# Expert gates for two of four quarters fetched from DRAM instead of spread by TensorE, in a convolution, attention and expert block

## What is computed

```python
logits = tokens @ router_w.T
probs = softmax(logits)
rw, re = top_k(probs, 2);  rw = rw / rw.sum(-1)
combine = zeros(N, 8);  combine[arange(N), re] = rw
for e in range(8):
    h = gelu(tokens @ w1[e] + b1[e])
    y = h @ w2[e] + b2[e]
    out = out + combine[:, e:e+1] * y
```

## Time and profile before

| what | value |
|---|---|
| median of three runs | 1167.22 us |
| the profiled execution, its own time | 1171.15 us |
| its span in the profile | 1169.3 us |
| TensorE busy | 1100.4 us, 94% |
| VectorE busy | 909.2 us, 78% |
| ScalarE busy | 611.7 us, 52% |
| GpSimd busy | 146.7 us, 13%, nothing of it in stage 3 |
| mean DMA rate | 68 GB/s |
| chain that ended last | TensorE 79%, ScalarE 8%, VectorE 6% |

### The profile page before, as it was taken

How to read it: one execution, slowest core, us unless ns; L and a number is a source line. 1 busy time by engine, 2 the same in 40 slices (tenths; PEclk the granted TensorE clock), 3 DMA queues, 4 the chain that set the end, 5 groups by cost and what they waited for, 6 DMA issues and landing times.

```text
span 1169.3 us, 28068 instructions
## 1 busy us (share of the span) xinstructions
PE 1100.4 (94%) x9550; PEld 739.6 (63%) x9550; DVE 909.2 (78%) x2575; ACT 611.7 (52%) x975; POOL 146.7 (13%) x173
## 2 busy tenths in 40 slices
PE   7858999999999999998789999999999999999998
PEld 7836777777777777777554555555555555555553
DVE  6943678888888888888678887887777777887875
ACT  0014566666666666665245555555555555555553
POOL 6021222222222222222100000000000000000000
PEclk9957899999999999999569999999999999999999
DMA  9501112122121212111012222222222222222221
GB/s 285 212 16 33 49 49 62 52 60 55 57 57 56 58 50 61 53 57 41 24 47 60 67 71 70 67 68 70 71 66 67 71 71 67 68 70 69 67 67 48
DMA packets 136196, 79.18 MB, mean 68 GB/s; under 512 B 112417, under 2 KB 134177, under 8 KB 135345
## 3 DMA queue, kind: packets, MB, share of 16 engines
q1 hardware_dynamic: 127040, 64.78, 21.3%
q10 hardware_dynamic: 8064, 12.85, 2.9%
q0 software_dynamic: 1008, 0.43, 0.2%
HBM read 52.33 MB, written 25.69 MB: 67 GB/s over the span
## 4 chain that ended last, share of the span: by engine, by line
PE 79%; ACT 8%; DVE 6%; issue 3%; SPq 2%; DMA 1%; POOL 0%; DVEq 0%; ACTq 0%; POOLq 0%
PE p L1096 16%; PE p L1071 15%; PE p L1081 9%; PE p L1045 6%; PE p L916 5%; PE p L1011 5%; PE p L1023 4%; ACT prob L515 4%; PE p L909 4%; PE p L926 3%; ACT xt_s L459 3%; PE p L1040 2%; PE p L1092 2%; PE p L924 2%; DVE arena L603 1%
## 5 line engine op out<-in xcount | busy, mean ns | idle before, releaser
L532 ACT ACTIVATE arena<-p,b_s 128x896 f32<-128x896 f32 x224 | 225.3, 1007 | 246.9 <-PE p L1071 246.1
L825 DVE TENSOR_TENSOR arena<-arena,p 128x896 f32<-128x896 f32 x224 | 242.7, 1083 | 93.0 <-PE p L1081 89.8
L1096 PE MATMUL p<-arena,w_s 128*64 128x448 f32 x896 | 215.7, 560 | 0.3 <-DVE arena L825 0.3
L1071 PE MATMUL p<-thl,w_hi 128*128 128x448 f32 x448 | 164.9, 449 | 0.4 <-DVE thl L799 0.4
L1081 PE MATMUL p<-arena,selector 128*128 128x448 bf16 x448 | 124.7, 360 | 3.5 <-DVE arena L825 3.0
L1081 PEld LDWEIGHTS p<-arena,selector 128*128 128x128 bf16 x448 | 25.5, 97 | 161.6 <-issue 116.1
L1071 PE MATMUL p<-thl,w_lo 128*128 128x448 f32 x448 | 127.5, 366 | 0.0
L723 DVE TENSOR_REDUCE sm<-sq 128x14 f32<-128x896 f32 (+1 forms) x59 | 61.3, 1038 | 66.7 <-ACT sq L486 58.7
L1071 PEld LDWEIGHTS p<-thl,w_hi 128*128 128x128 f32 x448 | 85.8, 192 | 21.3 <-issue 1.0
L418 POOL TENSOR_TENSOR yb<-yb,bet 128x448 f32<-128x448 f32 x56 | 59.2, 1058 | 290.5 <-DVE xn_s L766 290.5
L1071 PEld LDWEIGHTS p<-thl,w_lo 128*128 128x128 f32 x448 | 85.0, 190 | 7.2
(11 more groups left out here) (174 smaller groups left out, 1793.8 us busy)
## 6 DMA issues: line engine op xcount, KB each, us to landing
tn_spill<-tnt_s ACTq DMA_DIRECT2D x56, 224.0 KB, 1.9
arena<-tn_spill SPq DMA_DIRECT2D x56, 224.0 KB, 3.4
t_s<-tn_spill SPq DMA_DIRECT2D x56, 224.0 KB, 2.5
arena<-in_x_dram SPq DMA_DIRECT2D x112, 96.0 KB, 2.1
out_dram<-arena SPq DMA_DIRECT2D x112, 96.0 KB, 1.8
resid<-in_x_dram SPq DMA_DIRECT2D x6, 1568.0 KB, 13.5
resid<-in_x_dram SPq DMA_DIRECT2D x6, 384.0 KB, 7.0
arena<-in_x_dram SPq DMA_DIRECT2D x112, 16.0 KB, 2.0
```

Of the source, the lines that this page charges most:

```text
L532: a.activation(hid[:, j % 2, :].rearrange("p (h n) -> p h n", h=H), (p34 if j % 2 == 0 else p56)[:, :, 0:CH], ACT.Gelu, bias=b1_s[:, j:j + ...
L825: v.tensor_tensor(gated[:, j % 2, :].rearrange("p (h n) -> p h n", h=H), hid[:, j % 2, :].rearrange("p (h n) -> p h n", h=H), p01[:, :, 0: ...
L1071: last = t.matmul(bank[:, h, 0:CH], w[:, 128 * j:128 * (j + 1)], thl[:, c, h, :], start=(k == 0), stop=(k == 1))
L1096: last = t.matmul(p2[64 * h:64 * h + 64, 0:CH], w2_s[:, j, :], gated[:, j % 2, h * CH:(h + 1) * CH], start=False, stop=(j == 3))
```

## The change

- Routing writes `comb` with the block index innermost (`k e b` in place of `t e`), so that for each group the nine columns of experts stand as 63 contiguous columns (expert, block).
- For each image pair, TensorE turns `comb` (`turn_gates`: seven matmuls with the identity, into `p01`), ScalarE copies it to the new tile `turned` and writes it to the new DRAM tensor `shares` (`spill_gates`: two copies, two DMAs). A row of `shares`, one for each group and expert, holds its 896 gates. Seven pairs are turned in the last seven steps of stage 2, the eighth in front of group 5.
- For units 1 and 3 the gate tile is loaded: `gates_in`, two transfers, each of which reads one row of 3,584 bytes for 64 partitions. `gates[1]` and `gates[3]` are single tiles. `spread` is left out for these units; VectorE multiplies `hid` by the loaded tile, in two instructions of 768 and 128 columns.
- `low` moves from VectorE to GpSimd.
- SyncE's step becomes: `gates_in(g - 1, 3)`, tokens of g, rows of g, `gates_in(g, 1)`, store of g - 2.

```diff
+    shares = nc.dram_tensor("gate_spill", (G, EM, NB * 128), f32).ap()
...
+        gates = {1: yb_tail[:, 0:H * CH], 3: tn_s[:, 0:H, :, :].rearrange("p s b c -> p (s b c)")}
+        turned = sb("turned", [128, 512])
...
+            def tokens_in(g, c):
+                wait(sp, s_hi, g - 1)
+                wait(sp, s_lo, g - 1)
+                sp.dma_start(tn_in[:, c, :].rearrange("p (h n) -> p h n", h=H),
+                             spill[g].rearrange("(h p) n -> p h n", h=H)).then_inc(s_ti[c], 16)
+            def gates_in(g, j):
+                wait(sp, s_gm, 4 * (g - 1) + j + 1)
+                for e in range(2):
+                    sp.dma_start(gates[j][64 * e:64 * e + 64], shares[g, 2 * j + e].partition_broadcast(64)).then_inc(s_gi[j], 16)
+            def store(g, c):
+                wait(sp, s_fin, g + 1)
...
+            def step3(g, c):
+                gates_in(g - 1, 3)
+                tokens_in(g, c)
+                rows(g, c)
+                gates_in(g, 1)
+                store(g - 2, c)
...
+            sp.wait_ge(s_gd, 32 * (NP - 1))
+            gates_in(1, 1)
+            for g in range(2, 8):
+                step3(g, g % 2)
+            sp.wait_ge(s_gd, 32 * NP)
+            with sp.Fori(4, G // 2) as i:
+                for c in range(2):
+                    step3(i * 2 + c, c)
...
+            def low(g, c):
+                wait(pool, s_lo, g)
+                wait(pool, s_hi, g + 1)
+                v.tensor_tensor(thl[64:128, c], tn_in[:, c].rearrange("p (h n) -> p h n", h=H),
+                                thl[0:64, c].bitcast(f32), ALU.subtract).then_inc(s_lo, 1)
...
+            def spill_gates(im):
+                act.wait_ge(s_gt, im + 1)
+                wait(act, s_gd, 32 * im)
+                for h in range(2):
+                    r, n = slice(64 * h, 64 * h + NB * EM), (CPI + 1 - h) // 2 * 128
+                    last = a.activation(turned[r, 0:n], p01[r, 1, 0:n], ACT.Copy)
+                last.then_inc(s_gts, 1)
+                act.wait_ge(s_gts, im + 1)
+                for h in range(2):
+                    n = (CPI + 1 - h) // 2
+                    act.dma_start(shares[im * CPI + h:(im + 1) * CPI:2]..., turned[...]...).then_inc(s_gd, 16)
...
             for c in range(7):
                 step(G + c, c, lambda d, c=c: d > c)
+                spill_gates(c)
...
             step3(3, 1, lambda d: True, 1)
-            with act.Fori(2, G // 2 - 1) as i:
+            step3(4, 0, lambda d: True, 2)
+            spill_gates(NP - 1)
+            step3(5, 1, lambda d: True, 2)
+            with act.Fori(3, G // 2 - 1) as i:
...
             def gate(g, c, j):
                 u = g * 4 + j
                 wait(dve, s_g, u + 1)
-                wait(dve, s_c, u + 1)
                 wait(dve, s_l2, u - 1)
-                v.tensor_tensor(gated[:, j % 2, :]..., hid[:, j % 2, :]..., p01[:, :, 0:CH], ALU.mult).then_inc(s_gm, 1)
+                if j in gates:
+                    wait(dve, s_gi[j], 32 * (g + 1))
+                    ...
+                    v.tensor_tensor(to[:, :, 0:TAIL]..., of[:, :, 0:TAIL]..., gates[j][:, 0:2 * TAIL]..., ALU.mult)
+                    v.tensor_tensor(to[:, :, TAIL:], of[:, :, TAIL:], gates[j][:, 2 * TAIL:]..., ALU.mult).then_inc(s_gm, 1)
+                else:
+                    wait(dve, s_c, g * 2 + j // 2 + 1)
+                    v.tensor_tensor(...).then_inc(s_gm, 1)
...
                             if more:
                                 parts_step(g + 1, 1 - c, 4)
-                                low(g + 1, 1 - c)
...
+            def turn_gates(im):
+                pe.wait_ge(s_comb, im + 1)
+                wait(pe, s_gts, im)
+                for k in range(CPI):
+                    at = (im * CPI + k) * NB * EM
+                    last = t.matmul(p01[64 * (k % 2):64 * (k % 2) + NB * EM, 1, k // 2 * 128:(k // 2 + 1) * 128],
+                                    comb[:, at:at + NB * EM], eye[:, :], start=True, stop=True)
+                last.then_inc(s_gt, 1)
...
             def spread(g, c, j):
-                wait(pe, s_gm, u)
+                wait(pe, s_gm, u - 1)
...
-                    if has(0):
+                    if has(0) and j not in gates:
                         spread(g, c, j)
...
             for c in range(7):
                 step(G + c, c, lambda d, c=c: d > c)
+                pe.wait_ge(s_ys, G)
+                turn_gates(c)
...
+            pe.wait_ge(s_gts, NP - 1)
             step3(0, 0, lambda d: d <= 0, first=2)
             step3(1, 1, lambda d: d <= 1)
+            for g in range(2, 5):
+                step3(g, g % 2, lambda d: True)
+            pe.wait_ge(s_gm, 4 * 4 + 3)
+            turn_gates(NP - 1)
+            pe.wait_ge(s_gts, NP)
+            step3(5, 1, lambda d: True)
+            with pe.Fori(3, G // 2 - 1) as i:
```

More of the change, by code:

```diff
@@ L228, in hybrid_kernel @@
         s_ct, s_cts, s_ctd = sem("comb_t"), sem("comb_t_copied"), sem("comb_t_doubled")
+        s_gt, s_gts = sem("gate_weights_turned"), sem("gate_weights_copied")
+        s_gd = sem("gate_weights_spilled")
+        s_gi = {j: sem(f"gates_in{j}") for j in (1, 3)}
         s_h, s_g, s_c, s_gm = sem("hidden"), sem("gelu"), sem("weights_spread"), sem("gated")
@@ L319, in rows @@
                 sp.dma_start(tn_rows[:, c, :], spill[g]).then_inc(s_tr[c], 16)
-            def step3(g, c, has):
-                if has(0):
[L323 to L332, removed]
+            def tokens_in(g, c):
[9 more added lines that the diff above has]
+                wait(sp, s_fin, g + 1)
+                for tile, tokens in pieces(out_tokens, g, fin[:, c, :]):
+                    sp.dma_start(tokens, tile).then_inc(s_out[c], 16)
+            def step3(g, c):
[4 more added lines that the diff above has]
+                store(g - 2, c)
             for c in range(2):
                 sp.wait_ge(s_sp[c], 16)
-                step3(c, c, lambda d: d == 0)
+                tokens_in(c, c)
+            sp.wait_ge(s_gd, 32)
+            sp.wait_ge(s_t2, G)
+            sp.wait_ge(s_tn, G)
+            gates_in(0, 1)
+            sp.wait_ge(s_s, G)
+            for c in range(2):
+                rows(c, c)
+            sp.wait_ge(s_tnt, G)
+            gates_in(0, 3)
             for k in range(3):
@@ L339, in _ @@
                 sp.wait_ge(s_sp[k], 16 * spilled)
-            sp.wait_ge(s_s, G)
-            sp.wait_ge(s_t2, G)
-            for c in range(2):
[L343 to L348, removed]
+            sp.wait_ge(s_gd, 32 * (NP - 1))
[4 more added lines that the diff above has]
+            with sp.Fori(4, G // 2) as i:
+                for c in range(2):
+                    step3(i * 2 + c, c)
+            gates_in(G - 1, 3)
+            for c in range(2):
+                store(G - 2 + c, c)
             for c in range(2):
@@ L436, in _ @@
             walk(pool, step, 7, G, 4, after)
+            def low(g, c):
[3 more added lines that the diff above has]
+                                thl[0:64, c].bitcast(f32), ALU.subtract).then_inc(s_lo, 1)
+            pool.wait_ge(s_zero, 3)
+            for c in range(2):
+                low(c, c)
+            with pool.Fori(1, G // 2) as i:
+                for c in range(2):
+                    low(i * 2 + c, c)
         @blk.scalar
@@ L883, in _ @@
                         parts_step(0, 0, k)
-                    low(0, 0)
             dve.wait_ge(s_comb, NP - 1)
```

32 lines of the change are left out of this document (17 added, 15 removed).

## The result

The changed kernel takes 1193.72 us (median of four runs, 1188.83 to 1195.58) where the kernel before takes 1167.78 (four runs, 1163.54 to 1168.40): 1.022 times as long, 95% interval 1.018 to 1.026, 26 us slower. The forecast was 1148 and faster; 1193.7 lies inside its range (1126 to 1202), near the end that belongs to rival B.

A forecast was written before the change was run, and what follows sets the result against it. TensorE was taken to bound stage 3 at 10.04 us a group, then a loop through SyncE's queue at 9.5. Saving 30 us in 56 groups less 11 spent once gave 1152 profiled, median 1148, range 1126 to 1202.

The forecast's parts named there:

- rival B: Gate transfers ahead of the tokens move at 210 GB/s: loop 0.9 longer, 10.4 us, median 1198; chance 0.2.
- The loop: Stage 3, gate 3 through SyncE's queue, tokens, `high`, gelu 2, gate 2 to the next gate 3: 9.5 us a group.
- point of no gain: Loop length of 9.84 us a group, reached with 0.65 of delay from the gates ahead of the tokens, not 0.3.
- End of gate 3 to the first issue: Loop term from VectorE's gate 3 to SyncE's first gate transfer issue: 0.1 us.
- Two issues of gate transfers: Loop term on SyncE's queue ahead of the tokens: 0.5 us each, 1.0 in all (0.8 to 1.4).
- Landing of the tokens and what the gates ahead of them add: Loop terms: 3.4 us from issue to landing, plus 0.3 (0 to 1.2) for gate transfers in the same rings.
- `high` to the end of gate 3: Loop term over ScalarE's `high` and gelu, gate 2, the `ct_s` copy and gate 3 in two pieces: 4.7 us.
- A removed spread: TensorE in stage 3: each of two spreads saves 0.48 us a group, taking 10.04 to 9.08.
- rival A: TensorE stays the bound, loop 8.7 us, group 9.2: 47 saved, 11 spent, median 1131; chance 0.2.
- Once-only costs: Gate turns and routing: 7 us entering stage 3, 2.3 for the eighth turn, 2 for routing; 11 together (5 to 16).
- Rival C: GpSimd's `low` and VectorE's two-SBUF-source gates block each other: 0.6 us wait, group 10.1, median 1181; chance 0.15.
- VectorE and GpSimd: Stage 3: VectorE's work sums to 7.2 us a group, not the bound; GpSimd's `low` takes 2.1, covered.

The follow-up runs named there:

- distinct rows: Changed kernel, each of a gate tile's 64 partitions reading its own row of x, not one shared gates row: 1173.2 us, 1.0077 of the kernel before.
- the loop opened: Changed kernel with SyncE asking for the tokens of g ahead of the gate transfers of g - 1, unit 3: 1165.1 us, 0.9999 of the kernel before.

## Why the prediction was wrong

**The loop was right, two of its terms were too small.** The prediction put the sum at 9.5 and the point of no gain at 9.84; it is 10.24 in the group shown and 10.39 on average. What failed is the stretch from the first gate issue to the landing of the tokens: 1.0 + 3.4 + 0.3 = 4.7 forecast, 5.4 measured in the group shown and 5.6 with the median landing. In the prediction's terms:

- *End of gate 3 to the first issue*: 0.1 forecast, 0.20 measured.
- *Two issues of gate transfers*: 1.0 forecast (0.8 to 1.4), 1.46 measured. An issue took 0.51 to 0.53, as taken from the plain one, but SyncE spends 0.2 on registers and waits between one issue and the next. The prediction had 0.60 for an issue with what stands between in its own row of four stores and took 0.5; even 0.60 would have given only 1.2, since the tokens' own wait comes on top.
- *Landing of the tokens and what the gates ahead of them add*: 3.7 forecast, 3.92 in this group and 4.1 at the median. So the gates add 0.7 to the 3.4 of before, where 0.3 was forecast; with distinct rows it is 0.4.
- *`high` to the end of gate 3*: 4.7 forecast, 4.66 measured. `high`, gelu, the copy and the pieces of 0.94 and 0.28 all came as forecast.

In the group shown the sum is 0.74 too small, and 0.46 of it is the issues. On average it is 0.89 too small, 0.46 for the issues and 0.4 for the landing. Neither alone slows the pace: with either taken off, 10.39 becomes 9.9 to 10.0, and the kernel before has 10.02.

The two terms are not independent. The prediction's own way of working out the delay, with 1.46 in place of 1.0 and its rate of 344 GB/s, gives no delay at all (the pair ends 3.05 after the first issue, the tokens reach full rate at 1.46 + 1.3 + 0.5 = 3.26) and a loop of 9.7. With rival B's 210 GB/s, which the windows bear out (212), the pair ends at 1.2 + 0.5 + 2.2 = 3.9, the delay is 0.64, and the loop 0.20 + 1.46 + 3.4 + 0.64 + 4.66 = 10.36. This is an estimate from these rows; no run took the issues and the rate apart. So rival B, with 10.4 and 1198, was nearer than its reason: the rate was its own, but distinct rows had it too, so the one row read 64 times isn't the cause of it; that row accounts for 0.3 at most. And its delay of 1.2 came out as 0.7, since the tokens were asked for later.

**A removed spread is worth 0.27, not 0.48.** The first term of the forecast, 9.08 for TensorE, took a record off the chain as if its neighbours kept their length. The run with two spreads out shows 9.49. So rival A, 1131, was out of reach: the best that a run of this change shows is the version with tokens first and `low` on VectorE, 0.53 a group over 49 groups, 26 saved and some 9 spent. That the forecast of 19 us less is near the 16 of that version is an accident: its loop of 9.5 is as long as TensorE's real group.

**Once-only costs**: 7 for the turn to stage 3, 2.3 for the eighth turn and 2 for routing were forecast, 11 in all. The changed kernel spent 5.0 on the way to group 2, and 2.2 from group 2 to 6 beyond the slower pace (3.7 less 4 x 0.37), 7.2 in all. The 3.6 and 5.2 of the run with that work alone add up to the same 9 as the first two terms, but by another split. The terms were not right one by one either. Every turn was priced at 1.8; of the seven before stage 3 five took 1.8 to 1.9 and two 1.04 and 1.07, at a granted clock of 1.00 from 585 to 590 where the kernel before had 0.50. And the chain holds a wait of 5.00 for a write of gate rows (from 589.27), which the forecast put at nothing.

**Rival C** was right in mechanism, not in its point of decision (`low` ending later than the copy of `ct_s`). In the changed kernel `low` ended at 913.11 and the copy at 913.58, so by that rule it was 0.5 from deciding. With the loop opened it took part of the gain although `low` ended at 912.40 and the copy began only at 914.13: it met unit 1's gate, which the prediction had not looked at. The piece lost 0.95 a group on average; without it the pace is 0.26 lower (9.75 to 9.49).

**VectorE and GpSimd**: neither became the bound. `low` took 2.09 on GpSimd (2.1 forecast), and 2.1 in the kernel before, where it cost nothing.

## What to carry to other kernels

When a load is put behind a wait for late work on an in-order queue, add up the whole round from that work back to itself. Take the time between issues from rows with several issues, not from single ones, and the rate of a burst from its first byte to its last, not from its best quarter of a microsecond. Put the load that closes such a round ahead of the wait: here one swap of two lines was worth 26 to 29 us, and with `low` back on VectorE the change turned from 26 us slower to 16 faster. A matmul taken off TensorE can give back less than its record, here 0.27 of 0.48, because the next one's record grows.

## What the runs showed that was not expected

- An instruction of VectorE with two SBUF sources, 128 columns, took 2.18 us beside GpSimd's `low` in place of 0.28: it ended 0.15 after GpSimd. The Trainium skill, SBUF — State Buffer, section SBUF: two separate sides, says that one of the two blocks the other for its whole instruction; these rows agree (912.40 and 912.55). A gate with one source in PSUM was not held: in the changed kernel it took 1.09 at 911.97, while `low` ran.
- One DRAM row read for 64 partitions: 0.3 us more for the transfer queued behind it than 64 distinct rows of x of the same size. Which resource the repeated row uses up was not tried. Three transfers of 64 partitions in a row moved at 212 GB/s with either kind of row. The rule of the Trainium skill that the prediction weighed (SBUF — State Buffer, section Door 1: The DMA port swizzle), by which 64 partitions move at half rate, would fit this mean and not the windows of 0.25 us at 344 and 358; no run loads the gates over 128 partitions, so none here tests it.
- Writes of 63 partitions in rows of 512 bytes, asked for by ScalarE, took long to complete in stage 2's last steps. The profile after shows ScalarE's next copy released by them, 5.4 us after their issue at 588.95:

```profile
588.95 0.77 ACTq L593 DMA_DIRECT2D gate_spill<-turned  x2
...
594.35 1.09 ACT L588 ACTIVATE turned<-p 63x512 f32<-63x512 f32 x2 [3.70 <-DMA gate_spill<-turned]
```

  The Trainium skill, DMA: Bandwidth & Descriptors, section Why a DMA increments its semaphore by 16 and not by 1, has a rule on how many of the sixteen engines a transfer is split over (the largest number up to 16 that divides the outer sizes), which would be nine for 63 partitions; no run here tests it.

- The first layer right behind a second layer (float32, 128*64) is 0.19 longer than behind a spread (bf16, 128*128): 1.00 and 0.81, in the chains of both kernels without the two spreads. The two differ in type as well as in shape, and which of these counts wasn't tried.
